# Attention on one core: the score products as four tiles of 32 stationary columns, each value product in one piece

## The chip, the cores and the metric

The kernel runs on one core of one Trainium2 chip. Time is device time in microseconds of one execution. TensorE (PE) multiplies matrices; its weight loads (PEld) are instructions of their own. VectorE is DVE, ScalarE is ACT, GpSimd is POOL, and SP issues most transfers. The engines run side by side and are ordered by semaphores alone.

## The reference, cut to what matters

A transformer block on x of 4 x 1024 tokens with 128 channels: attention with 16 heads of 8 channels, then a mixture of 8 experts. The part the change touches:

```python
q = _gelu(concatenate([q_c, q_r])).reshape(b, s, H, HD).transpose(0, 2, 1, 3)   # H = 16, HD = 8
k = _gelu(concatenate([k_c, k_r])).reshape(b, s, H, HD).transpose(0, 2, 1, 3)
scores = einsum('bhqd,bhkd->bhqk', q, k) * HD ** -0.5
scores = where(causal, -inf, scores)
attn = softmax(scores, axis=-1)
out = einsum('bhqk,bhkd->bhqd', attn, v)          # v is 8 channels wide
out = out.transpose(0, 2, 1, 3).reshape(b, s, E)
return out @ wo + bo
```

## The kernel before

**Three blocks.** The first normalizes x, makes q, k and v, and splits q and k into three bfloat16 parts, so that a score product contracts over 96 rows; at its end it takes the first 18 items of row maxima of group 0. The second, the attention, is unrolled: 16 groups (4 batches x 4 quarters of the heads), 4 heads in each. The third is the mixture of experts, which the change leaves alone.

**A group.** TensorE's order is written out by hand. A group has 10 steps (`STEPS`) of up to 512 columns of queries, and each step has 4 slots, one for each head. In each slot TensorE does, in this order:

- the score product of this head and step (line 1342): keys stationary (128 columns), queries moving. One or two matmuls; it goes to one of two banks of PSUM. ScalarE takes the exponential of it into `expT` (line 1137), and the product waits until the exponential two slots back is done;
- the items that a list puts at this slot (`item`). A "max" item is a score product the other way round, queries stationary (line 279), for a later group; VectorE takes its row maxima (line 290). Two such items can be outstanding. A "neg" item is a bfloat16 transpose with 48 stationary columns (line 1286), an "out" item is four float32 transposes with 128 (line 1292). A few more (`turn`, `project`, `xf`, `logits`, `ranks`, `base`: 19 in the attention) belong to the work behind the attention and use 128 stationary columns;
- after the second and the fourth slot, half of the value product of the step two before (`product`, line 1315). Its stationary operand is the values of one head, 9 columns wide (8 channels and a column of ones for the sum); the four heads lie at partitions 0, 32, 64 and 96 of the output, so that each is a tile of 32 columns of the array. The moving operand is `expT` in float32, in pieces of at most 256 columns. One float32 matmul is two records in the trace.

For each group the score products have 48 matmuls and the max items 48 more (24 of 512 columns, 8 each of 384, 256 and 128, in either set). A step's value product has 1, 2 or 3 pieces (20 in a group), each of 4 heads; the first half takes the larger half of the pieces. Eight steps of ten have two halves with work in them and two have one, so that a group has 18 halves and the kernel 288. GpSimd masks the diagonal tiles of `expT`, scatters token rows and splits the maxima.

**The queue.** A wait stands on an instruction, or before it as an instruction of the sequencer (the "EVENT_SEMAPHORE" of lines 1285, 1290 and 1304). What stands behind a waiting instruction on its engine waits too.

Of the kernel before, what the change touches and what calls it, by code (L numbers as in the profile page):

```python
# [19 lines left out]
BF16 = mybir.dt.bfloat16  # L20
# [18 lines left out]
GH = 4  # L39
# [74 lines left out]
LAG = 2  # L114
DIAGS = [[col for kt, q0, n, col in segs if q0 == kt * P] for _, segs in STEPS]
# [77 lines left out]
def block_kernel(nc, x_d, wq_d, wqs_d, bq_d, wk_d, wks_d, bk_d, wkv_d, bkv_d, wv_d, bv_d, wo_d, bo_d,  # L193
# [13 lines left out]
    with ExitStack() as top:  # L207
# [63 lines left out]
        def scores_for_max(pe, odd, g, which):  # L271

            hh, tiles = MAX_ITEMS[which]
            for qi, col in tiles:
                width = P * (qi + 1)
                for lo in range(0, width, CT):
                    hi = min(width, lo + CT)
                    at = 2 * CT * odd + col
                    last = nc.tensor.matmul(psw[:, at + lo:at + hi], qr[:, g % RING, hh, qi * P:(qi + 1) * P],  # L279
                                            kr[:, g % RING, hh, lo:hi], start=True, stop=True)  # L280
# [659 lines left out]
        with ExitStack() as two:  # L940
# [296 lines left out]
            def _(pe):  # L1237
# [20 lines left out]
                def item(p, kind, g, which, n):  # L1258
# [25 lines left out]
                    elif kind == "neg":  # L1284
                        pe.wait_ge(split, 10 * g + 5 * (which + 1))
                        nc.tensor.transpose(
                            psw[0:6 * QT, 2 * CT * odd:2 * CT * odd + P // 2].bitcast(BF16),
                            negs[:, g % 2, which].rearrange("p h s q -> p (h s q)"), identb[:]).then_inc(wide_ready, 1)
# [7 lines left out]
                def product(g, s, part):  # L1296

# [3 lines left out]
                    if part == 0:  # L1301
                        pe.wait_ge(exp_ok, GH * NS * g + GH * (s + 1))
                        if DIAGS[s]:
                            pe.wait_ge(masked, NDIAG * g + DIAG_UNTIL[s])
                        if first:
                            wait(pe, oT_ok, 2 * (g - 1) + half + 1)

# [3 lines left out]
                    cut = (len(pieces) + 1) // 2  # L1311
                    for i, (kt, q0, n, col) in list(enumerate(pieces))[slice(0, cut) if part == 0 else slice(cut, None)]:
# [6 lines left out]
                    if part == (len(pieces) > 1):  # L1319
                        last.then_inc(pv_done, 1)  # L1320

                def product_behind(g, s, part):
                    if s >= LAG:
                        product(g, s - LAG, part)
                    elif g > 0:
                        product(g - 1, s - LAG + NS, part)
# [6 lines left out]
                for g in range(G):  # L1333
                    items = of_group(g)
                    for s in range(NS):
                        for hh in range(GH):
# [4 lines left out]
                            for kt, q0, m, col in STEPS[s][1]:  # L1341
                                last = nc.tensor.matmul(ps[:, B_S + hh % 2, col:col + m],  # L1342
                                                        kr[:, g % RING, hh, kt * P:(kt + 1) * P],
# [621 lines left out]
```

## Time and profile before

| what | value |
| --- | --- |
| three runs | 921.4, 916.28 and 918.73 us; median 918.73 |
| span of the profiled execution, first to last instruction | 931.8 us |
| TensorE busy in the span | 758.3 us (81%), 5615 matmuls and 5615 weight loads |
| VectorE, ScalarE, GpSimd busy | 632.4, 514.0 and 338.3 us |
| attention, from the first score product after the last early maxima to the last value product | 106 to 658 us of the span |
| TensorE, VectorE, ScalarE busy in it | 508.66, 414.85 and 371.37 us of 552 |

The profiled execution has no time of its own beside its span, which is 13 us above the median of the runs. A busy TensorE is not TensorE at its peak: a matmul's record covers its way through the array too, so that records of matmuls that follow each other overlap. The distance between the starts of two of them is what the second one waited for the first.

### The profile page before, as it was taken

What the parts mean: (1) busy time and instruction counts of PE and PEld (TensorE: products, weight loads), DVE (VectorE), ACT (ScalarE), POOL (GpSimd) and SP (SyncE); (2) the same over time, 40 slices, a digit from 0 to 9 for tenths busy, and PEclk for the clock granted to TensorE, in tenths of its full rate; (3) what the DMA queues carried; (4) which work ended last, traced back from release to release, by engine and by line L of the source; (5) the groups of instructions that cost most, each with busy time, mean ns of one, the idle gap of its engine ahead of it and who ended that gap; (6) DMA issues with size and microseconds to landing.
All of it is one profiled execution on the core that took longest, in us unless ns stands there. A gap on an engine that the chain in (4) does not pass through costs nothing. (4 is left out here: it accounts for less than half of the span.)

```text
span 931.8 us, 17439 instructions
## 1 busy us (share of the span) xinstructions
PE 758.3 (81%) x5615; PEld 359.8 (39%) x5615; DVE 632.4 (68%) x1916; ACT 514.0 (55%) x1048; POOL 338.3 (36%) x517
## 2 busy tenths in 40 slices
PE   5886699999999899899999989899267589898900
PEld 2331233333343243243233324233056468787700
DVE  6998788787878778668779758873044436565556
ACT  3562267677668576467576656678145224344423
POOL 3773212222222331732321642231441605565532
PEclk9996599999999899889899979999679889999955
DMA  6469254313531432514414433011511224332172
GB/s 163 138 165 212 72 115 63 54 33 50 92 60 28 86 63 52 111 46 66 82 32 88 86 72 62 28 36 32 167 49 58 63 70 129 94 86 67 55 203 79
DMA packets 112346, 77.07 MB, mean 83 GB/s; under 512 B 44202, under 2 KB 95819, under 8 KB 112075
## 3 DMA queue, kind: packets, MB, share of 16 engines
q1 hardware_dynamic: 99408, 63.02, 31.1%
q0 software_dynamic: 4352, 8.99, 2.9%
q10 hardware_dynamic: 8498, 3.97, 1.7%
q8 instruction: 46, 0.75, 0.4%
q14 instruction: 42, 0.34, 0.1%
HBM read 46.89 MB, written 26.56 MB: 79 GB/s over the span
## 5 line engine op out<-in xcount | busy, mean ns | idle before, releaser
L1137 ACT ACTIVATE expT<-ps 128x512 f32<-128x512 f32 (+1 forms) x640 | 334.0, 553 | 180.9 <-PE ps L1342 165.9
L290 DVE CUSTOM_DVE_ANT_0 x_in<-ps,mask 128x1024 bf16<-128x1024 f32 (+7 forms) x512 | 365.4, 755 | 93.7 <-PE ps L279 82.1
L1342 PE MATMUL ps<-q_space,k_space 96*128 96x512 bf16 (+3 forms) x768 | 227.1, 339 | 17.5 <-issue 10.0
L279 PE MATMUL ps<-k_space,q_space 96*128 96x512 bf16 (+3 forms) x768 | 203.1, 351 | 34.3 <-DVE mx L290 26.6
L1315 PE MATMUL ps<-expT,vr 128*9 128x256 f32 (+1 forms) x2560 | 183.4, 369 | 2.0 <-POOL expT L1098 2.0
L1098 POOL TENSOR_SCALAR_AFFINE_SELECT expT<-expT 128x512 f32<-128x512 f32 x128 | 81.7, 651 | 239.0 <-ACT expT L1137 239.0
L1342 PEld LDWEIGHTS ps<-q_space,k_space 96*128 96x128 bf16 x768 | 62.4, 99 | 172.6 <-ACT expT L1137 90.6
L279 PEld LDWEIGHTS ps<-k_space,q_space 96*128 96x128 bf16 x768 | 66.3, 101 | 101.1 <-DVE mx L290 61.8
L1524 POOL DMA_INDIRECT expert_rows<-row_ring,tile_to x72 | 69.1, 960 | 74.0 <-issue 40.1
L1315 PEld LDWEIGHTS ps<-expT,vr 128*9 128x9 f32 x2560 | 41.7, 89 | 101.0 <-issue 59.1
L705 POOL DMA_INDIRECT sorted_rows<-rows,places x64 | 62.9, 983 | 40.3 <-DVE places L890 22.5
L1058 POOL TENSOR_SCALAR negs<-mx 128x16 bf16<-128x16 f32 x32 | 8.2, 256 | 142.6 <-DVE mx L290 131.0
L1600 ACT ACTIVATE k_space<-ps 128x512 f32<-128x512 f32 x36 | 21.5, 597 | 54.5 <-PE ps L1879 38.9
L1755 DVE TENSOR_TENSOR k_space<-k_space,ps 128x512 f32<-128x512 f32 x36 | 24.8, 688 | 34.1 <-ACT k_space L1600 29.1
L1896 PE MATMUL ps<-w_gu,k_space 128*128 x288 | 41.5, 287 | 2.9 <-DVE k_space L1762 2.9
L290 DVE DVE_READ_ACCUMULATOR2_ANT mx<- 128x1 f32 x512 | 42.6, 83 | 0.0
L1896 PEld LDWEIGHTS ps<-w_gu,k_space 128*128 128x128 f32 x288 | 34.8, 191 | 10.4 <-issue 10.4
L1877 PE MATMUL ps<-w_hi,rows_hi 128*128 x72 | 34.8, 483 | 4.1 <-issue 2.7
L1798 PE MATMUL ps<-rows_hi,w_hi 128*128 128x512 f32 x32 | 15.5, 485 | 27.7 <-issue 26.9
L1762 DVE COPY k_space<-ps 128x512 f32<-128x512 f32 x36 | 24.9, 692 | 18.5 <-PE ps L1885 17.3
L1659 DVE TENSOR_TENSOR k_space<-k_space,ps 128x512 f32<-128x512 f32 x16 | 11.0, 687 | 33.8 <-PE ps L1800 25.1
L1608 ACT ACTIVATE row_ring<-ps,row_ring 128x128 f32<-128x128 f32 x72 | 22.6, 366 | 17.9 <-PE ps L1896 14.7
(194 smaller groups left out, 951.7 us busy)
## 6 DMA issues: line engine op xcount, KB each, us to landing
q_space<-q_parts SPq DMA_DIRECT2D x48, 192.0 KB
row_ring<-sorted_rows SPq DMA_DIRECT2D x72, 65.0 KB
k_space<-k_parts SPq DMA_DIRECT2D x32, 128.0 KB
q_parts<-parts SPq DMA_DIRECT2D x24, 128.0 KB, 2.3
k_parts<-parts SPq DMA_DIRECT2D x24, 128.0 KB, 2.8
k_space<-k_parts SPq DMA_DIRECT2D x16, 192.0 KB
v_ones<-v_st SPq DMA_DIRECT2D x8, 288.0 KB, 3.4
vr<-v_ones SPq DMA_DIRECT2D x16, 144.0 KB
```

The costliest lines, as they stand in the source:

```text
L279: last = nc.tensor.matmul(psw[:, at + lo:at + hi], qr[:, g % RING, hh, qi * P:(qi + 1) * P], kr[:, g % RING, hh, lo:hi], start=True, stop= ...
L290: last = nc.vector.tensor_tensor_reduce(out=unread[:, odd, col:col + width], in0=psw[:, 2 * CT * odd + col:2 * CT * odd + col + width], in ...
L705: nc.gpsimd.indirect_dma_start(out=xs_d, out_offset=bass.IndirectOffsetOnAxis(ap=pos[:, q, k, t:t + 1], axis=0), in_=xs[:, t // NT, k, t % ...
L1098: nc.gpsimd.affine_select(out=tile, in_=tile, compare_op=ALU.is_ge, fill=0.0, base=0, pattern=[[0, GH], [1, P]], channel_multiplier=-1).th ...
L1137: act.activation(expT[:, (NS * g + s) % PTN, hh, 0:width], ps[:, B_S + hh % 2, 0:width], ACT.Exp, scale=SCALE).then_inc(exp_ok, 1)
L1315: last = nc.tensor.matmul(ps[32 * hh:32 * hh + VW, B_O + half, at:at + n], vr[:, g % RING, kt, hh * VW:(hh + 1) * VW], expT[:, (NS * g + s ...
L1342: last = nc.tensor.matmul(ps[:, B_S + hh % 2, col:col + m], kr[:, g % RING, hh, kt * P:(kt + 1) * P], qr[:, g % RING, hh, q0:q0 + m], star ...
L1524: nc.gpsimd.indirect_dma_start(out=y_d, out_offset=bass.IndirectOffsetOnAxis(ap=to[:, r, i:i + 1], axis=0), in_=yt[:, r, i], in_offset=Non ...
L1755: v.tensor_tensor(hu[:, q % 2].rearrange("p (i n) -> p i n", i=2), gs[:, q % 2].rearrange("p (i n) -> p i n", i=2), ps[:, b:b + 2, INTER:] ...
L1762: v.tensor_copy(hT[:, q % 2], ps[:, B_HT]).then_inc(hT_ok, 1)
L1877: nc.tensor.matmul(out, hi, wide_hi[:, bass.ds(at, 2 * INTER)], start=True, stop=False)
L1896: last = nc.tensor.matmul(out, hT[:, q % 2, INTER * i + P * f:INTER * i + P * (f + 1)], wide_down[:, bass.ds(at + P * f, P)], start=f == 0 ...
```

## The change

Each score matmul (lines 279 and 1342) becomes four, one after the other: 32 of its 128 stationary columns each, the same moving operand, and the output in the 32 partitions that belong to them. The "neg" transpose becomes two, of 32 and 16 columns. The value product of a step is made whole after the second slot, not in halves after the second and the fourth.

```diff
+COLS = 32
+PV_AT = 1
@@ scores_for_max
-                    last = nc.tensor.matmul(psw[:, at + lo:at + hi], qr[:, g % RING, hh, qi * P:(qi + 1) * P],
-                                            kr[:, g % RING, hh, lo:hi], start=True, stop=True)
+                    for j in range(0, P, COLS):
+                        last = nc.tensor.matmul(psw[j:j + COLS, at + lo:at + hi],
+                                                qr[:, g % RING, hh, qi * P + j:qi * P + j + COLS],
+                                                kr[:, g % RING, hh, lo:hi], start=True, stop=True)
@@ item, "neg"
-                        nc.tensor.transpose(
-                            psw[0:6 * QT, 2 * CT * odd:2 * CT * odd + P // 2].bitcast(BF16),
-                            negs[:, g % 2, which].rearrange("p h s q -> p (h s q)"), identb[:]).then_inc(wide_ready, 1)
+                        for lo in range(0, 6 * QT, COLS):
+                            hi = min(6 * QT, lo + COLS)
+                            last = nc.tensor.transpose(
+                                psw[lo:hi, 2 * CT * odd:2 * CT * odd + P // 2].bitcast(BF16),
+                                negs[:, g % 2, which].rearrange("p h s q -> p (h s q)")[:, lo:hi], identb[:])
+                        last.then_inc(wide_ready, 1)
@@ product(g, s, part) becomes product(g, s)
-                    cut = (len(pieces) + 1) // 2
-                    for i, (kt, q0, n, col) in list(enumerate(pieces))[slice(0, cut) if part == 0 else slice(cut, None)]:
+                    for i, (kt, q0, n, col) in enumerate(pieces):
...
-                    if part == (len(pieces) > 1):
-                        last.then_inc(pv_done, 1)
+                    last.then_inc(pv_done, 1)
@@ the loop over slots
-                                last = nc.tensor.matmul(ps[:, B_S + hh % 2, col:col + m],
-                                                        kr[:, g % RING, hh, kt * P:(kt + 1) * P],
-                                                        qr[:, g % RING, hh, q0:q0 + m], start=True, stop=True)
+                                for j in range(0, P, COLS):
+                                    last = nc.tensor.matmul(ps[j:j + COLS, B_S + hh % 2, col:col + m],
+                                                            kr[:, g % RING, hh, kt * P + j:kt * P + j + COLS],
+                                                            qr[:, g % RING, hh, q0:q0 + m], start=True, stop=True)
...
-                            if hh % 2:
-                                product_behind(g, s, hh // 2)
+                            if hh == PV_AT:
+                                product_behind(g, s)
```

## Rows read from the trace of the kernel before

**Rows 1.** The page: span, busy time, and the forty slices (tenths).

```profile
span 931.8 us, 17439 instructions
...
PE 758.3 (81%) x5615; PEld 359.8 (39%) x5615; DVE 632.4 (68%) x1916; ACT 514.0 (55%) x1048; POOL 338.3 (36%) x517
...
PE   5886699999999899899999989899267589898900
...
PEclk9996599999999899889899979999679889999955
```

**Rows 2.** Busy time by stretch: four groups' time, then all sixteen groups.

```profile
core 0: us, PE busy (x) PEld busy (x) DVE busy (x) ACT busy (x) POOL busy (x), PEclk, DMA share, GB/s
...
182.00:215.00 33.00, 32.33 (x300) 12.10 (x299) 26.02 (x76) 23.64 (x46) 7.91 (x21) 1.00 0.40 64
...
sum 132.00, PE 127.85 PEld 46.70 DVE 109.36 ACT 91.23 POOL 31.84; mean PE 31.96 PEld 11.68 DVE 27.34 ACT 22.81 POOL 7.96
...
106.00:658.00 552.00, 508.66 (x4374) 190.17 (x4373) 414.85 (x1297) 371.37 (x740) 168.72 (x334) 0.95 0.33 64
```

**Rows 3.** TensorE matmuls by line and shape, whole execution.

```profile
L1315 PE MATMUL ps<-expT,vr 128*9 128x256 f32 x2048 | 163.6, 393 | 2.0 <-POOL expT L1098 2.0
L279 PE MATMUL ps<-k_space,q_space 96*128 96x512 bf16 x384 | 146.4, 413 | 25.2 <-DVE mx L290 19.1 <-DMA q_space<-in_const 4.3 <-PEq L308 1.4
L1342 PE MATMUL ps<-q_space,k_space 96*128 96x512 bf16 x384 | 146.0, 397 | 13.7 <-issue 10.0 <-ACT expT L1137 0.7 <-DMA q_space<-negT 0.7
```

**Rows 4.** Timeline of matmuls: start, us to the last end, line, count.

```profile
198.48 0.38 PE L1342 MATMUL ps<-q_space,k_space 96*128 96x384 bf16 x2
198.80 0.62 PE L1315 MATMUL ps<-expT,vr 128*9 128x256 f32 x8
199.35 0.28 PE L1342 MATMUL ps<-q_space,k_space 96*128 96x256 bf16 x1
```

**Rows 5.** The same view where transposes lie between score matmuls.

```profile
184.08 0.60 PE L1292 MATMUL ps<-identf,oT 128*128 128x128 f32 x4
184.62 0.24 PE L1286 MATMUL ps<-identb,negs 128*48 128x128 bf16 x1
184.78 0.39 PE L1342 MATMUL ps<-q_space,k_space 96*128 96x512 bf16 x1
...
191.67 0.39 PE L1342 MATMUL ps<-q_space,k_space 96*128 96x512 bf16 x1
191.89 0.60 PE L1292 MATMUL ps<-identf,oT 128*128 128x128 f32 x4
192.33 0.38 PE L1342 MATMUL ps<-q_space,k_space 96*128 96x512 bf16 x1
```

**Rows 6.** Weight loads: timeline of one product, then groups by shape.

```profile
198.79 0.12 PEld L1315 LDWEIGHTS ps<-expT,vr 128*9 128x9 f32 x8 [0.21 <-issue]
...
L279 PEld LDWEIGHTS ps<-k_space,q_space 96*128 96x128 bf16 x768 | 66.3, 101 | 101.1 <-DVE mx L290 61.8 <-issue 12.2 <-DVE negT L1170 0.3
...
L1315 PEld LDWEIGHTS ps<-expT,vr 128*9 128x9 f32 x2560 | 41.7, 89 | 101.0 <-issue 59.1 <-ACT expT L1137 35.0
...
L921 PEld LDWEIGHTS ps<-gate_scaled,rows_turned 128*128 128x128 f32 x64 | 7.7, 191 | 2.3 <-DVE mx L290 1.2 <-ACT rows_turned L736 0.9
```

**Rows 7.** Timeline of matmuls with full-width float32 weight loads.

```profile
340.77 1.06 PE L921 MATMUL ps<-gate_scaled,rows_turned 128*128 128x8 f32 x8
```

**Rows 8.** Timeline of matmuls where two value products follow each other.

```profile
654.79 1.49 PE L1315 MATMUL ps<-expT,vr 128*9 128x256 f32 x32
```

**Rows 9.** Two waits of TensorE's sequencer by line, between 213 and 215 us.

```profile
L1290 PEldq EVENT_SEMAPHORE  x1: 51/51/51, 213.8 to 213.8; - x1
...
L1285 PEldq EVENT_SEMAPHORE  x1: 51/51/51, 213.9 to 213.9; - x1
```

**Rows 10.** Waits from 116 to 248 us: total, times, longest.

```profile
ACT expT L1137 <- PE ps L1342: 39.2, 74, 2.0
...
DVE x_in L290 <- PE ps L279: 14.7, 30, 1.0
```

More of the change, by code:

```diff
@@ L1294, in item, with product @@
                         last.then_inc(wide_ready, 1)
-                def product(g, s, part):
+                def product(g, s):
                     half, segs = STEPS[s]
                     first, end = s in (0, HALF0), s in (HALF0 - 1, NS - 1)
[L1301 to L1306, printed above, removed]
+                    pe.wait_ge(exp_ok, GH * NS * g + GH * (s + 1))
+                    if DIAGS[s]:
+                        pe.wait_ge(masked, NDIAG * g + DIAG_UNTIL[s])
+                    if first:
+                        wait(pe, oT_ok, 2 * (g - 1) + half + 1)
                     pieces = [(kt, q0 + o, min(CT // 2, n - o), col + o) for kt, q0, n, col in segs
                               for o in range(0, n, CT // 2)]
-                    cut = (len(pieces) + 1) // 2
-                    for i, (kt, q0, n, col) in list(enumerate(pieces))[slice(0, cut) if part == 0 else slice(cut, None)]:
+                    for i, (kt, q0, n, col) in enumerate(pieces):
                         at = q0 - CT * half
@@ L1318, in product, with product_behind @@
                                 stop=end and i == len(pieces) - 1)
-                    if part == (len(pieces) > 1):
-                        last.then_inc(pv_done, 1)
-                def product_behind(g, s, part):
+                    last.then_inc(pv_done, 1)
+                def product_behind(g, s):
                     if s >= LAG:
-                        product(g, s - LAG, part)
+                        product(g, s - LAG)
                     elif g > 0:
-                        product(g - 1, s - LAG + NS, part)
+                        product(g - 1, s - LAG + NS)
                 for p, e in enumerate(WIDE):
@@ L1348, in _ @@
                                     item(p, *rest)
-                            if hh % 2:
-                                product_behind(g, s, hh // 2)
+                            if hh == PV_AT:
+                                product_behind(g, s)
                 for s in range(NS - LAG, NS):
-                    for part in range(2):
-                        product(G - 1, s, part)
+                    product(G - 1, s)
                 item(len(WIDE) - 1, *WIDE[-1][2:])
```

## The prediction

> **What bounds the kernel now.** The page first: TensorE is busy 81% of the span and, over slices 6 to 28, the attention, mostly nine tenths and more, at a clock that is mostly the full one [rows 1]. Then the busy time by stretch. In four clean groups of 33 us each TensorE is busy 127.85 of 132 us (97%), VectorE 83%, ScalarE 69%; over all sixteen groups (552 us, 34.5 a group) the shares are 92, 75 and 67% [rows 2]. The reader is to see that TensorE sets the pace there, with VectorE next. The waits say the same: in the clean stretch ScalarE waits for score products 39.2 us and VectorE for max products 14.7 us [rows 10], while the matmuls themselves are rarely late: in all 2.0 us idle before value products, 25.2 and 13.7 us before the widest score matmuls, early stages included [rows 3].
>
> But a busy record is not a working array. The timeline by starts shows what lies between. A score matmul of 512 columns lets the next start after 0.22 us (191.67 to 191.89) [rows 5]. Of the value product, eight records in 0.62 us are one piece of 256 columns in all four heads [rows 4], and 32 records in 1.49 us are 768 columns [rows 8]: 0.87 us for 512 columns more, so 0.435 us a piece of 256. The four heads do run side by side. Now the ways in and out: from 198.48 to 198.80 go 512 columns of scores, 0.32 us where 0.22 would do; from 198.80 to 199.35 goes one piece, 0.55 us where 0.435 would do [rows 4]. So each half of a value product loses 0.10 us on the way in and 0.115 us on the way out, in which the array does nothing.
>
> What causes it? Not the change of type: from a bfloat16 score product to float32 transposes, both with 128 stationary columns, and back again, starts follow without a gap (191.67, 191.89, then 0.44 us for four transposes to 192.33). But where a transpose with 48 stationary columns follows, 0.10 us is lost before it (184.08 plus 0.44 is 184.52, it starts at 184.62), and of the 0.16 us behind it about 0.11, since its 128 moving columns need 0.05 [rows 5]. So the loss comes with the width of the tile in which the array is used, and that is what the change makes equal.
>
> **What goes.** 288 halves by 0.215 us: 61.9 us. 32 neg transposes by 0.21 us: 6.7 us. In return, the 32 out items and the 19 items of the other work keep 128 columns and now stand between narrow ones: 51 by 0.21 us, 10.7 us. Net 57.9 us of TensorE's time.
>
> **What comes.** Three matmuls and three loads more for each of the 1,536 score matmuls, and one of either for each of 32 neg transposes: 9,280 instructions.
>
> First the stream. Four value tiles run side by side, each with a moving operand of its own, in float32 [rows 4, 8]. So four score tiles of 512 columns should take the 0.22 us of one, and I cost the matmuls of 384 and 512 columns at nothing in stream time; the cover is the stream of the other three tiles, and what it costs without that cover is a rival below.
>
> Then the loads. A load is hidden behind the matmul before it as long as that is longer. Full-width float32 loads show what an unhidden one costs: eight matmuls of 8 columns take 1.06 us to the last end, and less some 0.25 us for the last one's own length 0.81 us are left for seven, 0.115 us each [rows 7]; that is 0.9 ns a column, 0.03 us for 32. Four of them in turn are 0.115 us, side by side 0.03 us. The value product's eight loads of 9 columns, 89 ns each, end within 0.12 us, so they start within 0.03 us [rows 6], where 72 columns in turn would take 0.065 us. So loads of different tiles overlap, at least of that size.
>
> Then the supply of instructions. Two waits of the sequencer, at lines 1290 and 1285, start 0.1 us apart, with eight instructions between them (four loads, four matmuls), and the first takes 51 ns of that [rows 9]. With the rounding this is below 0.15 us, at most 19 ns an instruction; taken as printed it is 6 ns. The eight of a narrow set of tiles are then 0.05 to 0.15 us.
>
> So only the narrow matmuls pay. A 128-column one needs 0.055 us now (a quarter of 0.22), and a set of four between 0.055 and 0.15 us; I take 0.095 us, about half way, as the loads may show in part and the supply lies near its lower value. 256 of them by 0.04 us: 10.2 us (0 to 24). A 256-column one needs 0.11 us now; I take 0.115 us for the 256 of them: 1.3 us (0 to 10). And a set's last tile starts about 0.02 us behind its first (eight loads took 0.03 [rows 6]), which an engine feels that waits for it: 104 such waits in 132 us [rows 10] are 435 in 552, by 0.02 us 8.7 us, of which I take half, 4.4 us (0 to 9). What comes is 16 us in sum (0 to 43).
>
> The Trainium skill (TensorEngine Tiling (Array Packing), Restrictions and Gotchas) has a rule that speaks against the change: column tiling switches the fast weight load off. This trace agrees that there are two kinds, 101 ns for a load of 128 bfloat16 columns and 191 ns for a float32 one [rows 6]. The page TensorE: Matmul & The Clock Gate of the same skill (LDWEIGHTS) gives 27 ns for 32 columns without it, an estimate of 107 ns for four in turn; by that the 256 narrowest matmuls would cost 13 us, where I have 10.
>
> **The product in one piece.** Where nothing is lost at its ends it matters little whether it comes in 288 halves or 160 wholes. Its waits (exponentials of the step two before, the mask) are passed at the second slot, as now. Behind it stand two score products and their items, later by half a product (0.435 us); its end comes two slots earlier, and so does the release of `expT`'s buffer to ScalarE. I cost it at nothing: ScalarE has 33% idle and VectorE 17 to 25% [rows 2] in which to catch up within a step. What it costs if that cover is gone is a rival.
>
> **The sum.** TensorE is relieved of 57.9 less 16, 42 us (15 to 58) of 552. How much of it reaches the end? VectorE's 415 and ScalarE's 371 us stay [rows 2]. In the clean groups 7.6% less makes 30.5 us of 33, and VectorE's 27.34 us are 90% of that. Engines that hand each other pieces of up to a microsecond through two buffers will not run so without new waits, and what TensorE loses now, it will then in part wait for. I take 70% as what arrives: 29 us. On the profiled execution that is 903 of 931.8; its span lies 13 us (1.4%) above the median of the runs, and 918.7 less 28.6 is 890 us.
>
> **Rivals.**
>
> *VectorE takes over at once.* If TensorE's waits for VectorE take back all but a fifth, 8 us arrive: 911. For it: VectorE waits for max products only 14.7 of 132 us, the most it can win there, 11% [rows 10]. Against: that is still more than the 7.6% which TensorE gives.
>
> *The whole product starves the others: slower.* For 0.87 us TensorE makes no score and no max product, where it was 0.435 plus 0.215 us. One score and one item lie ready then, and either lasts its engine for about a slot, 0.8 us (33 us by 40). Eight steps of ten have such a product: 128 by up to 0.435 us, 56 us if all of it shows at the end. The kernel becomes slower from where 0.33 us of each shows (42 by 128); at the full price it takes 919 plus 14, 933. Against: both engines have idle time in each step now.
>
> *Supply.* At 31 ns an instruction a group's 556 pairs (384 for the score matmuls, 160 value, 12 others) would need 34.5 us, the whole present group, and nothing is won: 919 to 925. Against: at most 19 ns between two waits [rows 9], and 32 pairs in 1.2 us [rows 8], though those may have been queued ahead. The Trainium skill (TensorE: Matmul & The Clock Gate, Wait — 56ns, not 53.3ns?) knows such a case, about 62 ns a matmul where microcode decodes it.
>
> *Tiles in turn, or a lower clock: slower.* A group's score matmuls stream 15.8 us (36,864 columns by 0.22 us for 512), its value product 7.8 us. If the four tiles ran in turn it would take 47 us more a group, some 1,640 us in all; if the clock fell from 2.4 to 1.2 GHz 24 us more, some 1,260. For it: this trace has no score product in narrow tiles. Against: heads overlap [rows 4, 8], and in slices 27 and 28 value and score products alternate at nine tenths of the clock or more [rows 1].
>
> *The loss stays*, since every new set of tiles costs it anyway: then only 128 halves go, 27.5 us less the 16, at 70% 911 us.
>
> **The numbers.** Forecast (873 to 905) 0.70; VectorE takes over (905 to 917) 0.12; starved by the product 0.07; supply 0.04; tiles or clock 0.04; the loss stays 0.03. The range takes in the bounds of the costs and of the share that arrives, from 80% of 58 us to half of 15: 873 to 912, and it leaves out no more than the last 0.2. 0.5% (4.6 us) is about what these runs can tell from no change. Faster: 0.70, 0.07 of the second case and 0.03, 0.80. Same: 0.05 of the second and 0.02 of supply, 0.07. Slower: the rest, 0.13.
>
> **What would show it.** In the profile after: no 0.10 us between a score product's stream and the first value matmul, none behind the last; four score tiles of 512 columns that start within 0.03 us of each other, the next set 0.22 us later; sets of 128 columns 0.06 to 0.12 us apart; VectorE at 88% or more of a clean group, ScalarE's waits for score products shorter. I am wrong if sets of 512 columns lie 0.25 us or more apart, if VectorE waits longer for max products, or if the granted clock in the attention, 0.95 now [rows 2], drops.

## The result and the profile after

The changed kernel takes 924.86 us (median of 20 executions, 918.5 to 931.52). The kernel before takes 919.89 us (20 executions, 908.57 to 929.1). The medians stand as 1.005 to 1. The recorded ratio is 1.009, with a 95% interval from 1.0061 to 1.012; this one, like every ratio below, is formed from fast executions alone, those no more than 1.5% above the fastest of their kernel, which here leaves out the upper part of the wide spread of before. Either way the changed kernel is slower, by 0.5 to 0.9%, where I forecast 890 us.

The page of the profiled execution after the change (922.58 us by the clock of the runs, span 920.8):

```profile
span 920.8 us, 26719 instructions
PE 723.0 (79%) x10255; PEld 405.3 (44%) x10255; DVE 632.7 (69%) x1916; ACT 513.2 (56%) x1048; POOL 339.2 (37%) x517
...
PE   5786688999888898978898988888457789898900
...
PEclk9996599999999999999999989998869899999955
...
q8 instruction: 82, 1.34, 0.7%
...
L1345 PE MATMUL ps<-q_space,k_space 96*32 96x512 bf16 (+3 forms) x3072 | 236.0, 338 | 38.6 <-ACT expT L1141 34.7
```

Set beside [rows 1] the two spans mislead: 931.8 before, 920.8 after. They differ in the third block, which the change leaves alone: 276.4 us in the trace of before, 266.9 us in this one. That is nearly the whole difference. The record does not name the chips of these two traces; I take them for two, since the third block sorts the traces of known chips in the same way (see the lengths of the groups). So executions are timed against each other on one chip only, and traces are compared by stages.

What the page does show is that TensorE's row of tenths, mostly nines in the attention before, now has many eights, at nearly the same clock (0.96 in the attention, 0.95 before). TensorE has become less busy, and the time has not become shorter. Busy time by stretch, for three clean groups (90 us), for the stretch of [rows 2] and for the sixteen groups:

```profile
144.00:234.00 90.00, 82.23 (x1672) 40.84 (x1665) 72.74 (x209) 64.17 (x126) 22.01 (x54) 1.00 0.33 53
...
116.00:248.00 132.00, 117.90 (x2394) 57.91 (x2383) 109.36 (x320) 90.03 (x178) 32.40 (x80) 1.00 0.39 72
...
106.00:658.00 552.00, 475.45 (x8878) 236.63 (x8879) 414.77 (x1297) 371.06 (x741) 171.14 (x339) 0.96 0.34 65
```

Over the 132 us TensorE's busy time fell by 9.95 us (127.85 to 117.90), and over the attention by 33.2 (508.66 to 475.45). VectorE does in 132 us what it did before, 109.36 us in both traces: the pace of a clean group has not changed. TensorE was relieved and then stood idle for what it had gained. The waits of the same 132 us have not become shorter either:

```profile
ACT expT L1141 <- PE ps L1345: 40.6, 61, 1.6
...
DVE x_in L294 <- PE ps L282: 14.8, 31, 0.9
```

In [rows 10] they are 39.2 and 14.7 us. I had named VectorE at 88% and shorter waits of ScalarE as signs of being right; VectorE is at 83%, as before, and ScalarE waits 1.4 us longer.

The timeline of TensorE's matmuls shows both halves of the story:

```profile
182.43 0.40 PE L1345 MATMUL ps<-q_space,k_space 96*32 96x512 bf16 x4
182.66 0.44 PE L282 MATMUL ps<-k_space,q_space 96*32 96x512 bf16 x8
182.93 0.39 PE L1345 MATMUL ps<-q_space,k_space 96*32 96x512 bf16 x4
183.45 0.62 PE L282 MATMUL ps<-k_space,q_space 96*32 96x512 bf16 x8
183.89 1.04 PE L1318 MATMUL ps<-expT,vr 128*9 128x256 f32 x24
184.76 0.61 PE L1345 MATMUL ps<-q_space,k_space 96*32 96x512 bf16 x8
185.86 0.40 PE L1345 MATMUL ps<-q_space,k_space 96*32 96x512 bf16 x4 [0.48 <-ACT expT L1141]
186.19 0.66 PE L1299 MATMUL ps<-identf,oT 128*128 128x128 f32 x4
186.77 0.23 PE L1292 MATMUL ps<-identb,negs 128*32 128x128 bf16 x2
...
187.01 0.64 PE L1318 MATMUL ps<-expT,vr 128*9 128x256 f32 x8
187.45 0.42 PE L1345 MATMUL ps<-q_space,k_space 96*32 96x512 bf16 x4
```

Four tiles of 512 columns take 0.23 us (182.43 to 182.66), the time of one full-width matmul. A whole product of 512 columns (pieces of 256, 128 and 128) takes 0.87 us (183.89 to 184.76) and one of 256 takes 0.44 us (187.01 to 187.45), with nothing lost behind either, where [rows 4] had 0.55 us for the latter. The loss now stands at the full-width transposes: 0.33 us from a score set to the first of them (185.86 to 186.19), of which 0.11 is lost. Nor are the sets held up by their loads. The four loads of the set that starts at 182.93 start with the 128-column set before it, 0.05 us ahead:

```profile
182.88 0.11 PEld L1345 LDWEIGHTS ps<-q_space,k_space 96*32 96x32 bf16 x4
```

All this is as forecast, or better. But behind the product TensorE waits 0.48 us for ScalarE before the first score product of the next step. ScalarE over the same time:

```profile
183.02 1.10 ACT L1141 ACTIVATE expT<-ps 128x512 f32<-128x512 f32 x2
185.21 1.76 ACT L1141 ACTIVATE expT<-ps 128x512 f32<-128x512 f32 x3 [1.08 <-PE ps L1345]
```

It has done the step's first two exponentials at 184.12 and gets the third's scores, which stand behind the whole product, only at 185.2: 1.08 us idle. It then needs 0.55 us for each, and TensorE, which has made both remaining score products, has no bank left until the first of them is through. Each waits for the other in turn. The waits from 143.5 to 233.5 us (total, times, longest):

```profile
ACT expT L1141 <- PE ps L1345: 25.6, 40, 1.1
...
PEld ps L1345 <- ACT expT L1141: 18.0, 42, 1.0
PE ps L1345 <- ACT expT L1141: 5.9, 21, 0.5
...
DVE x_in L294 <- PE ps L282: 10.6, 24, 0.9
```

**Lengths of the groups.** In the experiments I read each trace by group: from the start of a group's first exponential to that of the next (the last group: to the end of its last exponential, from where on I count the third block, two value products included). Groups 1 to 3 are clean; groups 4 to 7, 9 to 11, 13 and 14 carry other work; 8 and 12 carry twelve scatters of rows each and the loads of attention rows. Each line is one profiled execution, in us. The last column says for how long the granted clock stood at the lower of its two levels (1.2 GHz, 0.5 in the profile) in the nine other groups and in group 15; in the clean groups it is the full 2.4 GHz in every trace.

| kernel | group 0 | clean, mean | nine others | 8 | 12 | 15 | attention | third block | lower clock |
| --- | --- | --- | --- | --- | --- | --- | --- | --- | --- |
| before (first trace) | 35.8 | 29.9 | 317.6 | 39.6 | 40.4 | 25.6 | 548.8 | 276.4 | 24, 0 |
| before_third | 36.1 | 29.9 | 309.4 | 39.2 | 39.6 | 27.0 | 541.2 | 280.9 | 0, 3 |
| before_fourth | 36.1 | 29.9 | 318.4 | 39.3 | 40.2 | 25.6 | 549.4 | 283.2 | 24, 0 |
| before_again | 35.7 | 29.9 | 317.8 | 39.3 | 39.7 | 27.0 | 549.4 | 278.5 | 24, 3 |
| after | 37.3 | 30.0 | 316.4 | 36.1 | 36.8 | 30.1 | 546.9 | 266.9 | 14, 7 |
| after_again | 36.9 | 30.0 | 314.9 | 45.6 | 47.7 | 30.1 | 565.3 | 283.7 | 7, 7 |
| after_fourth | 37.1 | 30.0 | 314.9 | 47.5 | 45.7 | 30.3 | 565.5 | 280.7 | 7, 7 |
| whole_wide | 38.1 | 31.5 | 322.4 | 37.9 | 35.7 | 28.5 | 557.2 | 267.5 | 3, 0 |
| tiles_halves | 35.8 | 27.6 | 308.7 | 36.4 | 37.0 | 24.9 | 525.6 | 266.5 | 20, 0 |
| halves_again | 35.6 | 27.8 | 308.1 | 45.8 | 47.0 | 26.2 | 546.1 | 282.6 | 14, 3 |
| tiles_quarters | 39.6 | 28.4 | 313.3 | 36.1 | 37.9 | 27.7 | 539.8 | 266.8 | 27, 7 |
| whole_at3 | 35.8 | 30.0 | 311.1 | 36.9 | 36.7 | 31.1 | 541.8 | 267.4 | 10, 10 |
| tiles64_halves | 36.0 | 30.3 | 323.4 | 43.1 | 43.0 | 29.8 | 566.3 | 276.3 | 20, 7 |
| halves_12 | 36.0 | 29.4 | 311.4 | 46.6 | 46.3 | 25.9 | 554.2 | 280.6 | 10, 0 |
| whole_more_dve | 37.2 | 30.1 | 316.2 | 45.0 | 46.7 | 30.3 | 565.7 | 277.3 | 14, 7 |
| halves_more_dve | 35.9 | 27.9 | 309.4 | 44.8 | 46.4 | 24.9 | 545.0 | 278.4 | 14, 0 |
| whole_more_act | 37.3 | 30.0 | 318.9 | 45.1 | 48.5 | 27.6 | 567.5 | 282.7 | 10, 0 |
| halves_more_act | 35.8 | 27.6 | 310.3 | 46.6 | 44.5 | 26.4 | 546.6 | 279.9 | 14, 3 |
| whole_act_third | 37.4 | 30.6 | 319.5 | 45.2 | 45.9 | 30.6 | 570.3 | 277.7 | 14, 7 |
| before_more_waits | 35.6 | 31.6 | 322.5 | 45.2 | 43.7 | 29.2 | 571.0 | 281.3 | 7, 3 |

The reader is to see three things. The clean groups of one kernel are alike on every chip (before 29.9 in every trace, after 30.0, the tiles with halves 27.6 and 27.8), so they can be compared between chips. The third block sorts the traces into two kinds of chip: 267 us in the four traces of one numbered chip and in the first of after, 276 to 284 us in all others, which come from four numbered chips and, in the first of before, from an unnamed one. The granted clock of the block differs too, 0.85 in the first kind and 0.81 to 0.84 in the second; what is cause there and what effect stays open. Groups 8 and 12 depend on the kind, and are compared only within one.

The third thing is the clock outside the clean groups. Three of the four traces of before have 24 us at the lower clock in the nine others and take 318 us for them; the fourth has none and takes 309.4: some 0.36 us longer for each us at the lower clock. Group 15 shows the same, 25.6 us at the full clock and 27.0 us with 3 us at the lower one. So these groups are to be compared at like clock.

### The profile page after: what moved, and what is told of

Same layout as the page of the kernel before. It is cut to its first block and busy times, and to the rows that moved or that the text cites. A ratio compares the mean times of both kernels' runs of the same rounds, so it can differ in the third digit from the quotient of the medians.

```text
span 920.8 us, 26719 instructions
## 1 busy us (share of the span) xinstructions
PE 723.0 (79%) x10255; PEld 405.3 (44%) x10255; DVE 632.7 (69%) x1916; ACT 513.2 (56%) x1048; POOL 339.2 (37%) x517
## 3 DMA queue, kind: packets, MB, share of 16 engines
q1 hardware_dynamic: 99408, 63.02, 31.6%
## 5 line engine op out<-in xcount | busy, mean ns | idle before, releaser
L1345 PE MATMUL ps<-q_space,k_space 96*32 96x512 bf16 (+3 forms) x3072 | 236.0, 338 | 38.6 <-ACT expT L1141 34.7
L282 PE MATMUL ps<-k_space,q_space 96*32 96x512 bf16 (+3 forms) x3072 | 206.0, 348 | 36.1 <-DVE mx L294 28.0
L1318 PE MATMUL ps<-expT,vr 128*9 128x256 f32 (+1 forms) x2560 | 158.7, 367 | 2.1 <-POOL expT L1102 2.1
L1345 PEld LDWEIGHTS ps<-q_space,k_space 96*32 96x32 bf16 x3072 | 76.9, 97 | 150.5 <-ACT expT L1141 89.5
L282 PEld LDWEIGHTS ps<-k_space,q_space 96*32 96x32 bf16 x3072 | 72.6, 99 | 101.9 <-DVE mx L294 68.3
L1526 POOL DMA_INDIRECT expert_rows<-row_ring,tile_to x72 | 68.9, 958 | 67.8 <-ACT row_ring L1610 46.7
L1318 PEld LDWEIGHTS ps<-expT,vr 128*9 128x9 f32 x2560 | 66.2, 92 | 56.1 <-issue 7.3
L1757 DVE TENSOR_TENSOR k_space<-k_space,ps 128x512 f32<-128x512 f32 x36 | 24.8, 688 | 34.6 <-ACT k_space L1602 34.6
L1898 PEld LDWEIGHTS ps<-w_gu,k_space 128*128 128x128 f32 x288 | 34.8, 191 | 10.3 <-issue 10.3
L1879 PE MATMUL ps<-w_hi,rows_hi 128*128 x72 | 34.9, 485 | 4.2 <-issue 2.7
L1764 DVE COPY k_space<-ps 128x512 f32<-128x512 f32 x36 | 24.9, 692 | 18.2 <-PE ps L1887 17.8
L1179 DVE RECIPROCAL rsum<-ps 128x16 f32<-128x16 f32 x32 | 8.2, 257 | 34.9 <-PE ps L1299 34.9
```

The source lines that it names most:

```text
L282: last = nc.tensor.matmul(psw[j:j + COLS, at + lo:at + hi], qr[:, g % RING, hh, qi * P + j:qi * P + j + COLS], kr[:, g % RING, hh, lo:hi], ...
L1318: last = nc.tensor.matmul(ps[32 * hh:32 * hh + VW, B_O + half, at:at + n], vr[:, g % RING, kt, hh * VW:(hh + 1) * VW], expT[:, (NS * g + s ...
L1345: last = nc.tensor.matmul(ps[j:j + COLS, B_S + hh % 2, col:col + m], kr[:, g % RING, hh, kt * P + j:kt * P + j + COLS], qr[:, g % RING, hh ...
L1526: nc.gpsimd.indirect_dma_start(out=y_d, out_offset=bass.IndirectOffsetOnAxis(ap=to[:, r, i:i + 1], axis=0), in_=yt[:, r, i], in_offset=Non ...
L1757: v.tensor_tensor(hu[:, q % 2].rearrange("p (i n) -> p i n", i=2), gs[:, q % 2].rearrange("p (i n) -> p i n", i=2), ps[:, b:b + 2, INTER:] ...
L1764: v.tensor_copy(hT[:, q % 2], ps[:, B_HT]).then_inc(hT_ok, 1)
```

## The experiments

### The two parts of the change, each alone

One chip, timed against before (median 920.85 us there). Of the edits the call alone is shown; where the product comes in parts, `product` takes a part as it did before.

**tiles_halves**: the narrow tiles, with the product in halves as before.

```diff
-                            if hh == PV_AT:
-                                product_behind(g, s)
+                            if hh % 2:
+                                product_behind(g, s, hh // 2)
```

> The score products as four tiles, the value product in two halves as before. Theory A (the loss at each change of tile width is gone, but the whole product of 0.87 us lets ScalarE and VectorE run dry, and TensorE then waits for them): 885 to 902 us, faster than before by 2 to 4%, and TensorE's waits for exponentials shorter than in the changed kernel. Theory B (a group's time is set by VectorE and ScalarE with the two buffers between them, whatever TensorE does): 915 to 926, as before, with a clean group at 30 us again.

Measured: 902.31 us, ratio 0.981 (0.9767 to 0.9852).

**whole_wide**: the kernel before, with the whole product after the second slot.

```diff
-                            if hh % 2:
-                                product_behind(g, s, hh // 2)
+                            if hh == PV_AT:
+                                product_behind(g, s)
```

> The score products with 128 stationary columns as before, the value product whole after the second slot. Theory A: 128 ways in and out fewer (27 us of TensorE's time), but all the starving that the changed kernel has: 925 to 945 us, slower than both. Theory B: 915 to 926.

Measured: 933.13 us, 1.0143 (1.0087 to 1.0199).

**whole_at3**: the changed kernel, its whole product after the fourth slot.

```diff
-PV_AT = 1
+PV_AT = 3
```

> The changed kernel with its whole value product after the fourth slot, not the second. Theory A: the same block of 0.87 us at another place, 918 to 932 us, a difference of under 0.7% to the changed kernel. A third theory, C (it is the place after the second slot that is bad, not the length): faster than 912.

Measured: 917.66 us, 0.9973 (0.9945 to 1.0001).

**tiles_quarters**: narrow tiles, pieces of 128 columns (PIECE), a quarter of the product after each slot.

```diff
-                              for o in range(0, n, CT // 2)]
+                              for o in range(0, n, PIECE)]
...
-                            if hh == PV_AT:
-                                product_behind(g, s)
+                            product_behind(g, s, hh)
```

> The score products as four tiles, the value product cut into pieces of 128 columns, a quarter after each of the four slots. Theory A: finer pieces let no engine run dry, 878 to 900 us, no slower than with halves. Theory B: 915 to 926.

Measured: 910.87 us, 0.9872 (0.9823 to 0.9921). Theory A, that the whole product makes the others run dry, had 885 to 902, 925 to 945, 918 to 932 and 878 to 900 us for the four: whole_wide lies inside, tiles_halves and whole_at3 lie 0.3 us outside, and the quarters missed by 11 us.

What follows: the two parts have opposite signs. The narrow tiles alone gain 1.9%, and the whole product alone costs 1.4%. Clean groups lie at 29.9 (before), 31.5 (whole only), 27.6 (tiles only) and 30.0 us (both). With halves the tiles gain 2.3 us a group; on top of them the whole product costs 2.4, and 1.6 without them. Between tiles_halves and after, both of the 267 us kind, 21.3 us of attention are made up of 7.2 (three clean groups), 7.7 (nine others), 5.2 (group 15) and 1.5 (group 0), with 0.5 given back in groups 8 and 12. But group 15 is not at like clock: after has 7 us at the lower level in it, tiles_halves has none. The group in tiles_halves, after, and whole_more_act (further below; it is after with 2.1 us more of ScalarE's work a group), which stayed at the full clock:

```profile
607.40:632.30 24.90, 22.74 (x385) 10.22 (x381) 7.38 (x36) 21.48 (x43) 4.91 (x9) 1.00 0.14 34
...
623.80:653.90 30.10, 25.57 (x395) 12.42 (x391) 7.38 (x36) 21.66 (x43) 5.23 (x9) 0.89 0.11 26
...
644.60:672.20 27.60, 23.02 (x397) 11.26 (x393) 7.41 (x36) 22.29 (x53) 5.30 (x9) 1.00 0.12 28
```

So at the full clock the whole product costs 2.7 us there, 0.34 us each, and the other 2.5 us go with the clock. In the 7 us before the clock fell in after (at 628.2 us) TensorE was busy 88% of the time; about the same place in whole_more_act has 90%, with no fall. Why it falls in one execution and not in the other, no run shows.

tiles_halves in the clean stretch, by busy time and then by waits (143.5 to 233.5 us, which takes in 8 us of group 4 here):

```profile
143.00:226.00 83.00, 80.66 (x1680) 40.38 (x1672) 71.81 (x211) 65.23 (x127) 22.11 (x54) 1.00 0.35 57
```

```profile
ACT expT L1141 <- PE ps L1350: 17.0, 39, 0.9
PEld ps L1350 <- ACT expT L1141: 12.0, 42, 0.6
...
DVE x_in L294 <- PE ps L282: 7.4, 19, 0.6
...
PE ps L1350 <- ACT expT L1141: 1.6, 7, 0.3
```

TensorE is busy 97% of the stretch, nearly as before the change (98% in the row of [rows 2] from 182 to 215 us), and not 91% as after it. ScalarE waits for scores about as often (39 times), but 0.44 us each and not 0.64, and TensorE waits less for ScalarE in return. Its timeline, a step with the halves apart:

```profile
151.12 0.62 PE L282 MATMUL ps<-k_space,q_space 96*32 96x512 bf16 x8
151.56 0.83 PE L1322 MATMUL ps<-expT,vr 128*9 128x256 f32 x16
152.22 0.61 PE L1350 MATMUL ps<-q_space,k_space 96*32 96x512 bf16 x8
152.65 0.39 PE L1322 MATMUL ps<-expT,vr 128*9 128x128 f32 x8
153.31 0.40 PE L1350 MATMUL ps<-q_space,k_space 96*32 96x512 bf16 x4 [0.27 <-ACT expT L1141]
```

The second half (152.65) lies where TensorE would otherwise wait for the step's third exponential. The product after the fourth slot keeps the clean group at 30.0 us: one long piece costs the same in either place. But the waits have moved. From 143.5 to 233.5 us whole_at3 has

```profile
PEld ps L1345 <- ACT expT L1141: 12.1, 32, 0.7
PEld ps L282 <- DVE mx L294: 9.6, 20, 0.6
```

where after has 18.0 us for ScalarE and 3.6 for VectorE in the same two rows. There TensorE waits more for VectorE's maxima and no more for ScalarE than tiles_halves does (12.0 us). The account given above, by way of the exponentials, is that of the product after the second slot. Quarters are 0.8 us slower than halves in a clean group; these runs do not say why, though they have 2,048 loads and as many matmuls more.

### How the loss depends on the width

**tiles64_halves**: tiles_halves with two tiles of 64 columns.

```diff
-COLS = 32
+COLS = 64
```

> As tiles_halves, but each score product as two tiles of 64 stationary columns (the neg transpose of 48 columns is again one), so that its width still differs from the value product's 32. If the loss lies at every change of width: 0.2 us for each half again, clean groups at 29.9 us and 915 to 925 us in all, as before. If it is enough that both are less than the whole width: clean groups at 27.6 us and 900 to 905 us, as with four tiles.

Measured: 952.85 us, 1.0229 (1.0181 to 1.0277). Its timeline:

```profile
181.48 0.62 PE L1322 MATMUL ps<-expT,vr 128*9 128x256 f32 x8
182.03 0.41 PE L1350 MATMUL ps<-q_space,k_space 96*64 96x512 bf16 x2
...
182.75 0.60 PE L282 MATMUL ps<-k_space,q_space 96*64 96x512 bf16 x4
183.28 0.84 PE L1322 MATMUL ps<-expT,vr 128*9 128x256 f32 x16
```

A product of 256 columns to the next scores is 0.55 us (181.48 to 182.03), the same as before the change, and two sets of 512 columns to the product are 0.53 us (182.75 to 183.28) where 0.43 would do. So the loss is paid between 64 and 32 columns too. What removes it is an equal width, not narrow tiles as such. That part of the theory holds. The clean group is 30.3 us, 0.4 more than before, and the 2.3 us that tiles_halves gains in one are gone. The whole kernel is slower than the 915 to 925 us I expected; groups 8 and 12, 43 us each, have a part in that, as shown below.

**before_again**, an unchanged kernel on the same chip: 935.76 us. Its clean groups are 29.9 us as expected, its span of 934.0 us is not: this chip is of the second kind.

> The kernel before once more, for a trace beside those of the experiments: clean groups at 29.9 us, and groups with the other work shorter than in the first trace, whose span of 931.8 us lies above all its timed runs: 33 to 38 us, a span of 908 to 922.

### Whose time sets the pace

If VectorE or ScalarE had taken over as the bound, work added to it would show in full. A memset of 112 ns follows each of the 24 maxima of a group (2.7 us), or an activation of 8 columns, 206 ns, each step's first exponential (2.1 us).

```diff
+            nc.vector.memset(pad_v[:], 0.0).then_inc(pad_ok, 1)
...
+                            if hh == 0:
+                                act.activation(pad_a[:], identf[:, 0:MORE], ACT.Exp).then_inc(pad_ok, 1)
```

> The changed kernel with a small write of 64 columns on VectorE after each row maximum (24 in a group, some 0.07 us each, 1.5 to 2.5 us a group). If VectorE sets the pace of a clean group with the whole product, the group becomes 1.5 to 2.5 us longer (31.5 to 32.5 us); if it is ScalarE and the scores, under 0.8 us.

> tiles_halves with the same small writes on VectorE. I expect VectorE to be nearer to setting the pace here: clean groups longer by 1.5 to 2.5 us (29.1 to 30.1). If TensorE still sets it, under 0.8 us (below 28.4).

> The changed kernel with one small activation of 8 columns on ScalarE after the first exponential of each step (10 in a group, some 0.2 us each, 2 us a group), right where TensorE is about to start the whole product. If ScalarE runs dry during the product and then sets the pace, part of it falls into time that was idle: clean groups longer by under 1 us. If ScalarE's own time sets the pace throughout, by 2 us (32 us).

> tiles_halves with the same small activations. ScalarE is busy some 22 of 27.6 us: if it has slack there, clean groups longer by under 0.8 us; if it sets the pace, by 2 us (29.6 us).

The added instructions, by group of instructions over two clean groups (whole_more_dve, then whole_more_act):

```profile
L304 DVE MEMSET pad_v<- 128x64 f32 x48 | 5.4, 112 | 0.0
```

```profile
L1148 ACT ACTIVATE pad_a<-identf 128x8 f32<-128x8 f32 x20 | 4.1, 206 | 0.0
```

Measured, in clean groups: with the whole product 30.1 and 30.0 us (30.0 without), with halves 27.9 and 27.6 (27.6 without). At most 0.3 of 2.7 us and nothing of 2.1 us appear. Each is one execution. Neither engine's total sets the pace, in either kernel. That halves_more_dve did not lengthen either I had not expected.

**whole_act_third**: the same activation behind each step's third exponential.

> whole_more_act with its small activation (0.2 us, 10 in a group) behind the third exponential of each step, not behind the first. Theory D (with the whole product TensorE and ScalarE take turns: product and third score, then third and fourth exponential, then the next step's scores, so that time behind the first exponential is free and time behind the third is not): clean groups longer by 1 to 2 us, 31 to 32. If ScalarE has slack everywhere: 30.0 us again.

Measured: clean groups 30.6 us (30.2, 30.2, 31.2), 0.5 more for 2.1 us added. This is less than I expected. The place may have been ill chosen: TensorE's wait ends with the third exponential itself, and the activation stands behind it. So no run shows that time added inside the loop appears in full.

**halves_12**: tiles and halves, with the halves after the second and the third slot.

```diff
-                            if hh % 2:
-                                product_behind(g, s, hh // 2)
+                            if hh in (1, 2):
+                                product_behind(g, s, hh - 1)
```

> tiles_halves with the halves after the second and the third slot, so that one score product and its item lie between them and none between the second half and the fourth slot. Theory D: the third score is made between the halves and ScalarE has it while the second half runs, so most of the loss is gone: clean groups at 27.6 to 28.6 us. If it is the product's place or its total that counts: 29.5 to 30.1.

Measured: clean groups 29.4 us. I expected nearly the time of halves two slots apart (27.6); it has most of the whole product's. So it isn't only the length of a piece: it matters that TensorE has something to do between the fourth score product and the next step's first. TensorE's waits before the first and the second score product of a step, worked out from the starts of the matmuls as means over the steps of the clean groups, are 0.28 and 0.08 us in after, 0.09 and 0.01 in tiles_halves, 0.09 and 0.19 in halves_12. After against tiles_halves that is 0.27 us a step, 2.7 for ten, where the group is 2.4 us longer; halves_12 has 0.18 a step more, 1.8 for ten, and is 1.8 us longer.

**before_third** and **after_again** ran beside it on that chip: 929.55 and 956.32 us, one execution each. The 24 us between their attentions are groups 8 and 12 with 14.5, the nine others with 5.5, the last with 3.1, the first with 0.8 and the clean ones with 0.4. The reading I had put up for it, the loss in the first and the last group and the rest the same within 3 us, did not come true.

> The kernel before, on the same chip as the next run, for a comparison group by group: clean groups 29.9, first group 35.8, last group 25.6 to 27.0 us.

> The changed kernel on the same chip: clean groups 30.0, first group 37.3, last group 30.1 us. If the loss of about 1% sits in the first and the last group, these two are 5 to 6 us longer than in the run before it and the groups between them the same in sum within 3 us.

### Groups 8 and 12

After the change these groups take 36 to 37 us on the first kind of chip and 45.6 to 47.7 on the other, where those of before take 39 to 40 (all traces of before are from the other kind). A stretch of group 8 in two executions on one chip, after_again and then before_third:

```profile
386.00:394.00 8.00, 2.50 (x43) 0.83 (x42) 0.67 (x3) 1.32 (x3) 6.17 (x7) 0.91 0.65 119
```

```profile
386.00:394.00 8.00, 5.51 (x28) 1.32 (x27) 3.38 (x10) 2.87 (x6) 3.46 (x4) 0.55 0.69 151
```

TensorE, VectorE and ScalarE nearly stand still for 8 us in after_again; in before_third they go on, though at a lower clock. The timeline of after_again there:

```profile
388.35 0.40 PE L1345 MATMUL ps<-q_space,k_space 96*32 96x512 bf16 x4 [1.03 <-issue]
...
391.30 0.60 ACT L1141 ACTIVATE expT<-ps 128x512 f32<-128x512 f32 x1 [3.00 <-remote]
...
391.95 0.40 PE L1345 MATMUL ps<-q_space,k_space 96*32 96x512 bf16 x4 [2.82 <-issue]
...
395.59 0.69 DVE L294 CUSTOM_DVE_ANT_0 x_in<-ps,mask 128x512 bf16<-128x512 f32 x1 [8.66 <-remote]
```

TensorE waits for nothing that the profile shows ("issue"), in a stretch full of scatters and row loads. The queue that brings the instructions moved 46 packets in the execution of before and 82 after. To see whether more instructions alone do this, **before_more_waits** is the kernel before with eight waits long fulfilled, which become four sequencer instructions, ahead of each of the 768 matmuls of the score products; its work is the same.

```diff
+MORE = 8
...
                             wait(pe, exp_ok, n - 1)
                             for kt, q0, m, col in STEPS[s][1]:
+                                for _ in range(MORE):
+                                    pe.wait_ge(zeroed, 1)
```

> The kernel before with four instructions more before each score product for the exponentials, waits of TensorE's sequencer on a semaphore that has long had its value: 3072 instructions (196 KB) to be fetched and no work. Theory E (in groups 8 and 12 TensorE runs out of instructions, since the fetch stands behind the scattered rows on the DMA engines, and a kernel with more instructions stalls longer): groups 8 and 12 longer by 3 us or more than in before_fourth beyond what the clean groups gain, as in the kernel with two tiles of 64, which has as many more. If the number of instructions doesn't matter: no more than the clean groups' difference, under 1.5 us. The waits themselves cost the sequencer 51 ns each, up to 0.2 us a slot, which may lengthen the clean groups too.

> The kernel before, on one chip with the three runs behind it: clean groups 29.9 us; groups 8 and 12 (those with 12 scatters of token rows and the loads of attention rows in them) at 39 to 40 us.

> The changed kernel on that chip. If the chip is one where block three takes some 277 us or more: groups 8 and 12 at 45 to 48 us and 1.5 to 3% slower than before; if it is one with 267 us: 36 to 37 us and 0 to 1% slower.

> tiles_halves on the same chip: clean groups 27.6 us. On a chip with 277 us in block three, groups 8 and 12 at 44 to 47 us and in all only 0 to 1.5% faster than before; on one with 267 us 1.5 to 2.5% faster.

Measured on one chip: before_more_waits 961.02 us (one execution), before_fourth 941.07 (one), after_fourth 953.8 with ratio 1.0214 (1.0134 to 1.0294), and halves_again, the kernel of tiles_halves, 932.33 with 0.9974 (0.9921 to 1.0026). The waits of before_fourth and then before_more_waits from 375 to 420 us, and a row of the latter's page:

```profile
PEld ps L1342 <- issue: 8.7, 13, 2.4
```

```profile
PEld ps L1345 <- issue: 11.2, 15, 6.2
...
DVE x_in L291 <- remote: 8.7, 1, 8.7
```

```profile
q8 instruction: 58, 0.95, 0.5%
```

With 58 packets for 46, groups 8 and 12 take 45.2 and 43.7 us where before_fourth has 39.3 and 40.2, and the same stall of 8.7 us on VectorE is back. The extra instructions cost 1.7 us in a clean group as well; the rest of the 9.4, some 6 us, belongs to these two groups. Beyond the clean groups' difference that is 4.2 us in group 8 and 1.8 in group 12, where I had asked for 3 in each, and it is one execution. tiles64_halves, which also has 58 packets, takes 43.1 and 43.0 us. So more instructions of TensorE seem to be enough for the stall. The clock has a part in the sum: the two groups have 31 us at the lower level in before_more_waits and 20 in before_fourth, which at 0.36 us each would be some 4 us, an estimate from the traces of before. That they come late because their fetch shares the DMA engines with the scatters is argued from the packets and the place, not shown. Why VectorE and ScalarE stand still too, whose instruction counts did not change, stays open.

## Why the prediction was wrong

**The step that failed** is "The product in one piece": "I cost it at nothing". It costs 2.4 us in each clean group, 0.30 us for each of its eight whole products of 512 columns, and 2.7 us in the last group at the full clock, 0.34 us each (tiles_halves against after and whole_more_act). The reason given, that ScalarE and VectorE have idle time "in which to catch up within a step", fails because idle time over a stretch is no slack on a cycle. Scores, exponential and the next scores in two banks form a loop; 0.87 us without a score product is longer than the exponential that lies ready (0.55 us), and the wait comes back to TensorE at the next step's first score product. That the whole product costs this is shown by edits in both directions. The loop is read from the timeline, and the waits of halves_12 fit it, though the theory missed that run beforehand. The added work on either engine shows one side of it: their totals have room. That the loop itself has none is not shown by a run.

**The rival "the whole product starves the others"** was the right one. I had put it at up to 0.435 us each, slower from 0.33 us, with 0.07 of chance. Its size was 0.30 in clean groups, just short of the point I had worked out. But that point was 42 us spread over 128 products, and the narrow tiles gave less than 42, as said below.

**What goes** was right in kind. The loss at changes of width is gone between scores and value products and stands at the full-width transposes. It is 0.10 and 0.115 us for 64-column tiles too.

**What comes** was too high where I could not see it. A narrow set of 512 and one of 128 columns take 0.27 us together (182.66 to 182.93), 0.22 and 0.055. I had 0.095 for the latter, so the 10.2 us for narrow matmuls are nothing. The formula of the Trainium skill (TensorE: Matmul & The Clock Gate, LDWEIGHTS) gave me 27 ns for 32 columns, an estimate of 107 ns for four loads in turn; the trace does not agree, as the four cost less than 55 ns a set. The Trainium skill's case of about 62 ns a matmul, with microcode decoding it (same page, Wait — 56ns, not 53.3ns?), is not seen either: four matmuls go in 55 ns. So the rivals of tiles in turn, of supply as a steady price and of a loss that stays are refuted; the clock in the attention is 0.96 where it was 0.95.

**How much arrives.** I took 42 us off 552, 2.6 us a group, and 70% of it. In clean groups, with halves, 2.3 us arrive, 88%. Over the whole kernel the tiles alone gain 1.9%, 17.5 of 920 us, where I had 29. In the groups with other work less arrives. At the full clock group 7 takes 34.2 us before and 32.8 in tiles_halves, group 11 the same, group 6 takes 35.7 and 34.8, and group 9 takes 34.0 and, in halves_again, 33.3: 0.7 to 1.4 us each, where I had counted on 2.6 us of relief and 70% of it. I had also read a clean group wrongly. The four stretches of 33 us in [rows 2] are no groups; from 116 to 248 us lie most of group 0, the three clean groups of 29.9 us and half of group 4.

**The sum again.** On one chip (before_fourth and after_fourth, 16.1 us in the attention): groups 8 and 12 +13.7, the last +4.7 (with 7 us at the lower clock for none), the first +1.0, clean groups +0.3, the nine others −3.5. There the loss is 2.1%. The −3.5 is a matter of the clock, since before_fourth has 24 us of these groups at the lower level and after_fourth 7; against before_third, which has none, the nine others were +5.5. At the full clock groups 7, 9 and 11 take 34.9 us after the change and 34.2, 34.0 and 34.2 before. So the changed kernel is a little slower there too, which the clock partly hid. On chips of the first kind groups 8 and 12 do not stall, but I have no trace of before from one. How the 0.5 to 0.9% of the first measurement divides stays open. VectorE did not take over: adding to it lengthens nothing.

The best version of those timed is tiles_halves: 1.9% faster on one chip, no difference on another (0.9974), where groups 8 and 12 (45.8 and 47.0 us for 39.3 and 40.2) take back what the tiles gain.

## What to carry to other kernels

Idle time of an engine over a stretch is no cover for a longer piece of work on its partner. Take the loop of waits through the buffers between them and ask whether each piece is shorter than what lies ready, and what work is left for the place where the loop would wait: two halves in neighbouring slots cost 1.8 us a group more here than two halves two slots apart. Where an array changes its tile width often, make widths equal, but count the instructions added against the stretches where transfers are dense. Time each half of a two-part change alone, since here one half's cost hid the other's gain of 1.9%. And compare stretches of two traces only at like granted clock.

## What the runs showed of the hardware

- A change between matmul widths costs 0.10 us in and 0.115 us out, for 128 and 32 columns and also for 64 and 32.
- Four tiles of 32 columns with loads of their own run side by side: 0.22 us for 512 moving columns, 0.055 us for 128.
- 3,072 more sequencer instructions (192 a group) cost 1.7 us a clean group, 9 ns each, and some 6 us more in the two groups with dense transfers (one execution).
- One program's granted clock differs between executions outside the clean groups: before has 24 us of its nine other groups at the lower level in three traces (318 us) and none in a fourth (309.4 us).
- Chips differ for one program: the changed kernel's third block takes 267 or 281 to 284 us, its groups 8 and 12 take 36 to 37 or 46 to 48 us.
